# Shared stage of a fused attention and mixture-of-experts kernel: held tokens second, routed rows added within the group, loads issued earlier

## The reference

```python
probs = jax.nn.softmax(logits, axis=-1)
top_w, top_i = jax.lax.top_k(probs, K)          # K = 2 of 8 experts
h = jax.nn.silu(g) * u                          # per expert, inner width 352
expert_out = jnp.einsum('besi,eih->besh', h, w_down)
moe_out = jnp.einsum('besh,bse->bsh', expert_out, combine)
sh = jax.nn.silu(x @ sw_gate) * (x @ sw_up)     # shared expert, inner width 1408
shared_out = sh @ sw_down
shared_gate = jax.nn.sigmoid(x @ shared_gate_w)
return moe_out + shared_out * shared_gate       # and the kernel's input x is added
```

## Time and profile before

| | us |
|---|---|
| median of three timed runs | 2041.2 |
| the profiled execution, its own time | 2043.55 |
| its span in the profile | 2041.7 |
| PE busy (share of the span) | 1917.3 (94%) |
| VectorE (DVE) busy | 1022.2 (50%) |
| ScalarE (ACT) busy | 705.0 (35%) |
| GpSimd (POOL) busy | 657.9 (32%) |
| mean granted PE clock, share of full | 0.976 |
| HBM traffic, mean over the span | 71 GB/s |

### The profile page before, as it was taken

One profiled execution on the slowest core, in us unless ns is written; L12 is line 12 of the kernel. 1 busy time (PEld: TensorE's weight loads), 2 busy tenths in 40 slices (PEclk: granted clock), 3 DMA queues, 4 the chain that ended last, 5 costly groups with the idle time before them and its releaser, 6 DMA issues. The chain is left out here.

```text
span 2041.7 us, 28543 instructions
## 1 busy us (share of the span) xinstructions
PE 1917.3 (94%) x10324; PEld 1413.6 (69%) x10325; DVE 1022.2 (50%) x1661; ACT 705.0 (35%) x1276; POOL 657.9 (32%) x476
## 2 busy tenths in 40 slices
PE   4999999999999769899999999889999999999995
PEld 2444444444444357799999999878888888888874
DVE  3777777777777259343444443243433324242434
ACT  1566666666666522232233332231010101010000
POOL 3577776677765526111111111100101001010101
PEclk9999999999999879899999999989999999999998
DMA  6786667667663062432333322252302112130204
GB/s 124 111 132 103 106 126 110 108 101 131 104 98 60 19 235 91 148 125 82 109 120 125 111 80 78 90 163 73 103 22 82 42 60 66 37 102 1 93 17 154
DMA packets 117886, 196.17 MB, mean 96 GB/s; under 512 B 11280, under 2 KB 43024, under 8 KB 117808
## 3 DMA queue, kind: packets, MB, share of 16 engines
q1 hardware_dynamic: 106768, 158.98, 34.7%
q0 software_dynamic: 11040, 36.18, 6.1%
HBM read 100.71 MB, written 43.25 MB: 71 GB/s over the span
## 5 line engine op out<-in xcount | busy, mean ns | idle before, releaser
L382 DVE TENSOR_REDUCE maxcol<-ps_m 128x1 f32<-128x512 f32 x512 | 342.4, 683 | 180.8 <-PE ps_m L525 172.6
L321 ACT ACTIVATE e<-ps_e 128x512 f32<-128x512 f32 x512 | 297.4, 597 | 190.9 <-PE ps_e L520 189.5
L1289 POOL DMA_INDIRECT s_chosen<-routed,s_slot_now x64 | 61.5, 961 | 619.5 <-DVE s_total L1393 608.2
L126 POOL TENSOR_TENSOR e<-e 128x2048 f32<-128x2048 f32 x64 | 224.9, 3515 | 98.8 <-ACT e L321 98.8
L1347 DVE TENSOR_TENSOR s_h_f<-s_silu,s_ps_u 128x512 f32<-128x512 f32 x77 | 53.0, 688 | 394.3 <-PE s_ps_u L1419 344.6
L520 PE MATMUL ps_e<-qside,kside 98*128 98x512 f32 x512 | 242.0, 475 | 8.8 <-ACT e L321 7.8
L520 PEld LDWEIGHTS ps_e<-qside,kside 98*128 98x128 f32 x512 | 96.5, 189 | 212.7 <-ACT e L321 175.5
L525 PE MATMUL ps_m<-kside,qside 97*128 97x512 f32 x512 | 216.4, 428 | 16.4 <-DMA qside<-row_mask 13.5
L1315 ACT ACTIVATE s_silu<-s_ps_g 128x512 f32<-128x512 f32 x77 | 46.0, 598 | 531.3 <-PE s_ps_g L1419 531.3
L1016 DVE TENSOR_TENSOR e_h_f<-e_silu,e_ps_h 128x256 f32<-128x256 f32 (+1 forms) x108 | 45.1, 418 | 249.7 <-ACT e_silu L857 249.7
L1430 PE MATMUL s_ps_y<-s_d_hi,s_h_hi 128*128 128x512 f32 x352 | 139.6, 396 | 9.0 <-DVE s_h_lo L1367 9.0
(11 more groups left out here) (233 smaller groups left out, 4276.0 us busy)
## 6 DMA issues: line engine op xcount, KB each, us to landing
routed<-e_y SPq DMA_DIRECT2D x36, 512.0 KB, 2.8
kside<-q_hi SPq DMA_DIRECT2D x64, 256.0 KB
qside<-qm_hi SPq DMA_DIRECT2D x64, 256.0 KB
x_f<-in_x SPq DMA_DIRECT2D x16, 512.0 KB, 3.8
kside<-q_lo SPq DMA_DIRECT2D x32, 256.0 KB
qside<-qm_lo SPq DMA_DIRECT2D x32, 256.0 KB
attn<-xo SPq DMA_DIRECT2D x32, 256.0 KB, 3.7
keep_rows<-attn SPq DMA_DIRECT2D x8, 1024.0 KB, 5.6
```

The lines of the kernel that those rows point to most:

```text
L126: eng.tensor_tensor(into, into, e[k + 1][:, heads, :], ALU.add).then_inc(done, 1)
L321: act.activation(e[kb][:, g, :], ps_e[g % 2][:, :], ACT.Exp, scale=SCALE).then_inc(e_done, 1)
L382: dve.reduce_max(maxcol[par][:, g * KB + kb:g * KB + kb + 1], ps_m[g % 2][:, :], AX.X).then_inc(max_done, 1)
L1289: pool.indirect_dma_start(out=chosen[k][s % 2][:], out_offset=None, in_=routed, in_offset=bass.IndirectOffsetOnAxis(ap=slot_now[:, k, s:s ...
```

## The change

- In the shared stage a *place* is a group's position in the order. Place 0 is tokens 512 to 1023, place 1 the held tokens (`HELD_AT`), places 2 to 7 the rest. The held place has its own functions on each engine.
- Held tiles have three buffers (`RING`), two of them the expert stage's `y`. SyncE loads the first three while place 0 runs, behind the weights' chunk 3, place 2's rows and place 0's residual tiles. The load of step t waits for the halves of step t - 3. Then come the held place's residual tiles, one behind each of the next four held loads. Halves of held step 0 are made before `add_down` of place 0, into the other pair of buffers (`pair_of`).
- `add_chosen` of a group runs within that group, at steps 5 to 8 (2, 3, 7, 8 in the held place), onto the residual. `add_down` comes last and takes the down product block by block (`y_last`), each block then being ready to store. GpSimd's gather waits for `chosen_used`.
- `load_ahead` is called in the expert stage behind `load(1)`. The wait for the last store of `routed` moves from SyncE in the expert stage to GpSimd in the shared stage.
- The identity matrix is built once, in the expert stage, and kept.
- At the start of the shared stage both ScalarE and VectorE split the gate and up half of chunk 0 first, then round x, then split its down half. PE waits for the gate and up half before an up product and for the down half before a down product.

The diff, cut to its core:

```diff
@@ -580,7 +580,7 @@
     def sem(name):
         return sems.enter_context(nc.semaphore("e_" + name))
 
-    ident = sb("ident", [P, P], f32)
+    ident = keep["ident"]
...
     h_lo = [sb(f"h_lo{n}", [P, ST], f32r) for n in range(NI)]
     zeros = sb("zeros", [P, SB, H], f32)
-    y = sb("y", [P, SB, H], f32)
+    y = keep["ahead"]["y"]
...
-    y_done, stored = sem("y_done"), sem("stored")
+    y_done, stored = sem("y_done"), keep["routed_stored"]
...
         load(1)
+        sp.wait_ge(a_wlo, SI)
+        sp.wait_ge(a_t_mm, HT)
+        keep["load_ahead"](sp)
         sp.wait_ge(filled, 16 * (NTILES - FEWEST))
         sp.wait_ge(bounds_done, 1)
 
...
         each_expert(sp, start, tile)
-        total = sp.value_load(keep["bounds"][0:1, NE:NE + 1], min_val=1, max_val=NTILES - 1)
         for n in range(2):
             sp.wait_ge(a_stored[n], 16 * ((SI - n + 1) // 2))
-        keep["load_ahead"](sp)
-        alone(sp, stored, 16 * total + 16, consts, 8)
...
     GT = 512
     GB = GT // P
-    HELD = 1
-    NG = NTOK // GT - HELD
+    HELD_AT = 1
+    NG = NTOK // GT
     TOPK = 2
+    ADD_AT = NI - GB - 2
+    HELD_ADDS = (2, 3, NI - 4, NI - 3)
+    NE = keep["bounds"].shape[1] - 1
...
-    h_up = [sb(f"h_up{n}", [P, GT], f32) for n in range(2)]
-    h_in = [sem(f"h_in{n}") for n in range(2)]
+    RING = 3
+    y = keep["ahead"]["y"]
+    h_up = [y[:, 0, :], y[:, 1, :], sb("h_up", [P, GT], f32)[:]]
+    h_in = [sem(f"h_in{n}") for n in range(RING)]
...
-    base, consts = sem("base"), sem("consts")
     w_hi, w_lo = sem("w_hi"), sem("w_lo")
     residual_in, stored = [sem(f"residual_in{n}") for n in range(GB)], [sem(f"stored{n}") for n in range(GB)]
     chosen_in = [sem(f"chosen_in{n}") for n in range(2)]
-    t_mm, g_mm, u_mm, y_mm = sem("t_mm"), sem("g_mm"), sem("u_mm"), sem("y_mm")
+    t_mm, g_mm, u_mm, y_mm, y_last = sem("t_mm"), sem("g_mm"), sem("u_mm"), sem("y_mm"), sem("y_last")
     xhi_done, xlo_done = sem("xhi_done"), sem("xlo_done")
     silu_done, h_done, hhi_done, h_split = sem("silu_done"), sem("h_done"), sem("hhi_done"), sem("h_split")
-    slot_done, scale_done, y_read, sum_done, out_ready = sem("slot_done"), sem("scale_done"), sem("y_read"), sem("sum_done"), sem("out_ready")
+    slot_done, scale_done, sum_done, chosen_used, out_ready = (sem(n) for n in (
...
-    def groups(eng, group):
+    def places(eng, group, held_group):
 
         group(0)
-        with eng.Fori(1, NG - 1) as g:
-            group(g)
+        held_group()
+        group(HELD_AT + 1)
+        with eng.Fori(HELD_AT + 2, NG - 1) as p:
+            group(p)
         group(NG - 1)
 
...
+    def alternates(p):
+        return isinstance(p, int) and p in (HELD_AT, HELD_AT + 1)
+
+    def pair_of(p, t):
+
+        return (t + (isinstance(p, int) and p == HELD_AT)) % 2
+
+    def more(p):
+        return not isinstance(p, int) or p + 1 < NG
+
+    def full(p):
+
+        return 0 if isinstance(p, int) and p == 0 else p - 1
+
+    def tokens(p):
+
+        return {0: HELD_AT, HELD_AT: 0}.get(p, p) if isinstance(p, int) else p
...
+        def load_residual(p, s):
+
+            upto(sp, stored[s], 16 * p)
+            sp.dma_start(total[s][:], x_v[bass.ds((GB * tokens(p) + s) * P, P), :]).then_inc(residual_in[s], 16)
+
+        def store_block(p, s):
+            sp.wait_ge(out_ready, GB * p + s + 1)
+            sp.dma_start(out_v[bass.ds((GB * tokens(p) + s) * P, P), :], total[s][:]).then_inc(stored[s], 16)
+
+        def exchange(p):
+            for s in range(GB):
+                if not isinstance(p, int) or p:
+                    store_block(p - 1, s)
+            for s in range(GB):
+                load_residual(p, s)
+
+        def load_held(t):
+            if t >= RING:
+
+                sp.wait_ge(h_split, NI * HELD_AT + t - RING + 1)
+            sp.dma_start(h_up[t % RING], held[t * P:(t + 1) * P, :]).then_inc(h_in[t % RING], 16)
+
+        def group(p):
+            if more(p):
+
+                sp.wait_ge(t_mm, HT * (full(p) + 1))
+                load_rows(sp, keep["ahead"], attn, tokens(p + 1 if not isinstance(p, int) or p else HELD_AT + 1))
+            exchange(p)
+
+        def group_held():
+            for s in range(GB):
+                store_block(HELD_AT - 1, s)
+            for t in range(RING, NI):
+                load_held(t)
+                if t - RING < GB:
+                    load_residual(HELD_AT, t - RING)
+
         for t in range(2, NI):
 
             sp.wait_ge(w_lo, 2 * (t - 1))
             load_chunk(sp, keep["ahead"], sw_gate, sw_up, sw_down, t)
...
+            if t == 3:
+                group(0)
+                sp.wait_ge(slot_done, 1)
+                for k in range(RING):
+                    load_held(k)
+
+        places(sp, lambda p: None if isinstance(p, int) and p == 0 else group(p), group_held)
         for s in range(GB):
-            sp.wait_ge(stored[s], 16 * (NG + 1))
+            store_block(NG - 1, s)
+        for s in range(GB):
+            sp.wait_ge(stored[s], 16 * NG)
...
-        pool.memset(ident[:], 0.0).then_inc(base, 1)
-        pool.wait_ge(base, 1)
-        pool.affine_select(out=ident[:], in_=ident[:], compare_op=ALU.not_equal, fill=1.0, base=0,
-                           pattern=[[-1, P]], channel_multiplier=1).then_inc(consts, 1)
-
-        def group(g):
+
+        written = pool.value_load(keep["bounds"][0:1, NE:NE + 1], min_val=1, max_val=keep["tiles"] - 1)
+        alone(pool, keep["routed_stored"], 16 * written + 16, t_mm, 1)
+
...
                 if not (isinstance(b, int) and b <= 1):
-                    alone(pool, out_ready, b - 1, consts, 1)
+                    alone(pool, chosen_used, b - 1, slot_done, 1)
...
-        def split(t):
+        def split_gu(t):
             act.wait_ge(raw_in[t % 2], 16 * 3 * (t // 2 + 1))
             act.activation(gu_hi[:, t], raw_gu[t % 2][:], ACT.Copy).then_inc(w_hi, 1)
+
+        def split_d(t):
             act.activation(d_hi[:, t], raw_d[t % 2][:], ACT.Copy).then_inc(w_hi, 1)
 
-        def group(g):
-            first = isinstance(g, int) and g == 0
+        def split(t):
+            split_gu(t)
...
+        def halves(p, t, of):
+            n, k = NI * p + t, pair_of(p, t)
+
+            upto(dve, y_mm, n if t == 0 and not alternates(p) else n - 1)
+            dve.tensor_copy(h_hi[k][:], of).then_inc(hhi_done, 1)
+            dve.wait_ge(hhi_done, n + 1)
+            dve.tensor_tensor(h_lo[k][:], of, h_hi[k][:], ALU.subtract).then_inc(h_split, 1)
...
+        def scales(p):
+
+            upto(dve, out_ready, GB * p)
+            of = bass.ds(GB * tokens(p), GB)
+            dve.tensor_copy(scale_now[:, 0:TOPK, :], keep["weight"][:, :, of]).then_inc(scale_done, 1)
+            dve.tensor_copy(scale_now[:, TOPK, :], keep["shared_gate"][:, of]).then_inc(scale_done, 1)
+            dve.wait_ge(scale_done, 2 * (p + 1))
...
+        def add_chosen(p, s):
+
+            b = GB * p + s
+            dve.wait_ge(residual_in[s], 16 * (p + 1))
+            dve.wait_ge(chosen_in[s % 2], 16 * TOPK * (2 * p + s // 2 + 1))
             dve.scalar_tensor_tensor(out=total[s][:], in0=chosen[0][s % 2][:], scalar=scale_now[:, 0, s:s + 1],
                                      in1=total[s][:], op0=ALU.mult, op1=ALU.add).then_inc(sum_done, 1)
             dve.wait_ge(sum_done, b + 1)
             dve.scalar_tensor_tensor(out=total[s][:], in0=chosen[1][s % 2][:], scalar=scale_now[:, 1, s:s + 1],
-                                     in1=total[s][:], op0=ALU.mult, op1=ALU.add).then_inc(out_ready, 1)
-
+                                     in1=total[s][:], op0=ALU.mult, op1=ALU.add).then_inc(chosen_used, 1)
+
+        def add_down(p):
+
+            dve.wait_ge(chosen_used, GB * (p + 1))
+            for s in range(GB):
+                if s < GB - 1:
+                    dve.wait_ge(y_last, (GB - 1) * p + s + 1)
+                else:
+                    dve.wait_ge(y_mm, NI * (p + 1))
+                dve.scalar_tensor_tensor(out=total[s][:], in0=ps_y[s][:], scalar=scale_now[:, TOPK, s:s + 1],
+                                         in1=total[s][:], op0=ALU.mult, op1=ALU.add).then_inc(out_ready, 1)
+
+        def group(p):
+            first = isinstance(p, int) and p == 0
+            f = full(p)
+            scales(p)
...
+                dve.tensor_tensor(h_f[:], silu[:], ps_u[:], ALU.mult).then_inc(h_done, 1)
+                dve.wait_ge(h_done, n + 1)
+                halves(p, t, h_f[:])
+                if ADD_AT <= t < ADD_AT + GB:
+                    add_chosen(p, t - ADD_AT)
+            if more(p):
+                x_low(f + 1)
+            if first:
+                held_halves(0)
+            add_down(p)
...
+        def held_halves(t):
+            dve.wait_ge(h_in[t % RING], 16 * (t // RING + 1))
+            halves(HELD_AT, t, h_up[t % RING])
+
+        def group_held():
+            scales(HELD_AT)
+            for t in range(NI):
+                if t:
+                    held_halves(t)
```

(47 more changed lines are left out.)

167 lines of the change are left out of this document (50 added, 117 removed).

## The result

The changed kernel takes **2009.8 us** in the median of four runs (2008.6 to 2012.0), against 2040.1 us for the kernel before on the same chip (four runs, 2037.2 to 2042.5). The ratio is 0.9849, with a 95% interval of 0.9833 to 0.9864. The forecast was 2008.3 us, in a range of 2002 to 2018.

The account below looks back on a forecast made before the run. TensorE, busy 94% of the span, bounds the kernel; savings come from time without matmuls or with slow ones. Hand-over -8.7, first step -0.4, tail -56.75, held place +32.9 give -32.95 us: 2008.3 us, range 2002 to 2018.

Parts of the forecast that it names:

- before X: Up to the start of the experts' last matmul (X): the moved loads cost 0 us, bounds 0 and 8.
- hand-over: From experts' last matmul (X) to first shared gate product (G): moved loads let G start earlier, gain 8.7 us.
- first step: First to second gate product (G to G2): chunk 2's wait and slow clock cost 2.8 us against 3.16, gain 0.4.
- end: 60.05 us become: Behind the last full group: only one block's add and its store remain, 3.3 us (bounds 2.8 and 4.5).
- held place behind group 0: Held tokens' eleven steps moved behind place 0: 29.92 us of PE plus 3.0 of stalls, 32.9 us.
- Loads moved into the expert stage: Behind load(1): 2.6 MB of loads cost 0 us, bounds 0 and 8; SyncE's 6 us of issuing are free.
- rival (a): Expert stage: the moved loads delay the first experts, price up to 8 us, 2013 us; chance 0.12.
- Cover of chunk 4: Place 0: chunks 3 and 4 with the burst are through by 1346, needed by 1351; 5 us of cover, no cost.
- Rival (b): Held place stays paced by transfers as in the tail, 39.4 us; price 7.4 us, 2016 us; chance 0.13.
- (c): Hand-over does not shrink because something unseen holds the engines at the barrier: +8.7 us, 2017 us; chance 0.05.
- (d): All cover holds, with no stall in the first step or the held place: 2003 us; chance 0.06.
- (e): Slower than before: place 0 paced by its chunks, clock staying at 1.2 GHz; up to +90 us, 2098; chance 0.04.

Follow-up runs that it names:

- loads_alone: Kernel before with one edit: load_ahead called behind load(1) in the expert stage; 2037.0 us, ratio 0.9974.
- late_loads: Changed kernel with load_ahead called again at the end of the expert stage's SyncE program; 2014.4 us, ratio 0.9867.
- held_last: Changed kernel with the held place last instead of second, keeping its buffers, early halves and adds within the place; 2010.1 us, ratio 0.9838.
- adds_early: Changed kernel with the routed adds at steps 0 to 3 of each full place instead of 5 to 8; 2011.6 us, one run.
- warm_burst: Changed kernel with silu 0 ahead of chunk 2's split, 24 unused transposes, and the rows, residual and held-tile burst behind chunk 6; 2003.7 us, one run.
- late_gather: Changed kernel with GpSimd's first gathers held until chunk 2 has landed; 2006.7 us, one run.
- gather_burst: Changed kernel with GpSimd's first gathers behind chunk 2 and the burst behind chunk 6; 2005.8 us, one run.
- all_three: Changed kernel with silu 0 ahead of chunk 2's split, 24 unused transposes, first gathers behind chunk 2 and the burst behind chunk 6; 2007.6 us, ratio 0.9834.
- warm: Changed kernel with silu 0 ahead of chunk 2's split and 24 unused transposes to keep PE busy; 2005.9 us, ratio 0.9837.
- whole_product: Changed kernel with add_down waiting for the whole down product instead of block by block; 2012.5 us, ratio 0.9853.
- warm_burst_timed: Same kernel as warm_burst, timed against the kernel before; 2003.7 us in the median of five runs, ratio 0.9820.

## Why the prediction came out right, step by step

The sum forecast -32.95 us of span and -33.5 were measured in the traces (-30.3 between medians). Its steps:

| step | forecast | measured |
|---|---|---|
| before X | 0 | -0.8 |
| hand-over, X to G | -8.7 | -8.8 |
| first step | -0.4 | +0.9 |
| end: 60.05 us become | 3.3 | 3.5 |
| held place behind group 0 | 32.9 | 31.8 |

The last two rows, 3.5 + 31.8 - 60.05, give -24.75; with the rows above them -33.45, and nothing is left over. That the sum fits to 0.5 us is in part luck: the first step was 1.3 us too cheap, the held place 1.1 us too dear, and X lay 0.8 us earlier by chance.

*Hand-over: right, and for the reason given.* loads_alone and late_loads show that neither the loads nor the rest (the wait for the store, the identity, the order of the splits) would have done it alone; the sum of the parts' single gains (4.1 and 0.6) would have missed it.

*Loads moved into the expert stage: right in time, wrong in one number.* Load(1)'s use came 11.91 us after its first issue, 11.70 before, and the loss of up to 8 us of rival (a) did not appear; it was 11.94 in loads_alone, also with the loads there, and 11.38 in late_loads without them. Each load of a chunk was to take half a microsecond of SyncE; but some single issues took 2.6 and 4.2 us, and the whole 12 us instead of 6:

```profile
816.72 0.43 SPq L696 DMA_DIRECT2D e_raw_g<-in_w_gate  x1
...
819.31 0.38 SPq L1126 DMA_DIRECT2D keep_rows<-attn  x1
...
820.33 2.60 SPq L1134 DMA_DIRECT2D keep_raw_gu<-in_sw_up  x1
822.96 4.15 SPq L1135 DMA_DIRECT2D keep_raw_d<-in_sw_down  x1
...
829.86 1.32 SPq L1135 DMA_DIRECT2D keep_raw_d<-in_sw_down  x1
...
828.63 1.38 ACT L809 ACTIVATE e_hi_g<-e_raw_g 128x1408 fp32r<-128x1408 f32 x1 [9.62 <-DMA e_raw_d<-in_w_down]
```

They end at 831.2 and the next load is issued at 835.1. The cover was the one the forecast named, but 4 us of it are left, not 9.

*First step: the term that was mis-sized, 2.8 us forecast and 3.9 measured (9.32 less 5.44).* Two causes were named, the clock and silu 0 behind the split of chunk 2, and both are there. The 3.16 us of before were read a little high: from start to start the two products took 8.44 us (G to G2), 3.00 over 5.44, so the step lost 0.9. What was wrong is the duration of chunk 2: it was taken as 5.18 us from the earlier trace rows, where GpSimd's gathers had been issued from 7 us before it on. Now they go out from 1324.3 to 1329.3, right ahead of chunk 2 at 1328.55. With them chunk 2 took 6.3 to 7.9 us from issue to use (6.5 in the changed kernel, 7.8 in held_last, 7.5 in adds_early, 7.9 in warm_burst), and without them 5.2 to 5.4 (late_gather, gather_burst, all_three). Where the gathers lie 7 us ahead, as before, it took 5.0 and 5.1 (late_loads, loads_alone). What decides between 6.3 and 7.9 stays open. That spread is also why G to G2 moves between 9.3 and 10.6 in kernels that do the same thing there. The Trainium skill (DMA: Bandwidth & Descriptors, section Issuing engines are not separate DMA queues) says that transfers issued by SyncE, ScalarE and GpSimd run on the same 16 engines; the trace agrees, with 1 to 2.7 us for chunk 2. The forecast had weighed such sharing for the expert stage only and did not carry it to the place where it decided.

*Cover of chunk 4: right in sign, too large.* It was given as 5 us, with the chunks through by 1346; chunk 4 was first used at 1348.89. Silu 2 ended at 1350.96 and PE wanted it at 1353.74, 2.8 us later. late_gather and warm spent them: PE 1.97 and 1.52 us idle for it.

*Held place: right, a little dear.* The forecast had 3.0 us of stalls, measured are 0.55 and 0.38 at its start, 1.3 with their restarts, and a third, small one at step 3, 1.85 in all over its 29.92 us. The residual reload was the largest term there, 1.2 us at step 3; it cost about 0.4 with its restart in the changed kernel and 1.35 in all_three, where it went out 1.6 us later. Rival (b), pacing by transfers at 39.4 us, is out. What the position itself is worth the forecast did not say; held_last showed that it costs 1.5 us.

*Tail: right.* 3.3 forecast, 3.5 measured. whole_product shows that block by block is worth 2.1 us of the time behind the last matmul.

*Rivals.* (c) and (d) are out by the hand-over and the first step; (e) never came near: the granted clock is 1.00, 2.4 GHz, from 1334 to the end.

## What to carry to other kernels

When a hand-over is shortened, follow the first steps behind it in turn: here the clock, one activation behind a split, one chunk behind gathers and another behind a burst each hid the next. The two cures tried alone gave -0.7 and 1.8 us, three together 3.4 (single traces, of which the first step moves by up to 1.2 us by chance). A duration read from a trace holds for the traffic around it; before using it, look at what the change places beside it in the same engines. Give loads that are needed now the queue ahead of a burst that is needed tens of microseconds later.

## What I had not expected of the hardware

- SyncE's issue of one 256 KB load took 0.4 to 0.6 us in most rows, but 2.60, 4.15 and 2.18 us behind load(1) and group 0's rows, while load(1) was still waited for (819.3 to 831.2 above). Issuing is not a fixed price.
- A PE stall of 2.94 us in held_last (1335.3 to 1338.2) was followed by a granted clock of 0.62 and 0.53 in the next two stretches of 2 us; one of 2.14 us in adds_early was not. That, not the held tokens' position, is where held_last lost 1.6 us between G2 and the third gate product. The clock can also go either way from one execution to the next: after the same 1.88 us of idle PE the clock fell in warm_burst_timed (0.50 from 1322 to 1324) and not in all_three.

The two stretches of held_last:

```profile
1338.00:1340.00 2.00, 1.80 (x5) 1.48 (x6) 1.97 (x4) 1.63 (x3) 0.00 (x0) 0.62 1.05 392
1340.00:1342.00 2.00, 2.00 (x7) 1.52 (x6) 1.97 (x4) 0.00 (x0) 0.00 (x0) 0.53 1.05 385
```
